# SP stores and loads k, then q, then the shift rows; a pair holds neighbouring heads; half of the output is normalised by one instruction

## The chip, the core and the metric

The kernel runs on one core of one Trainium2 chip. The metric is the device time of one execution in microseconds. The kernel before takes 1407.23 us, the median of 3 runs (1406.34 to 1412.29).

The engines have instruction queues of their own, which run in order and meet only at semaphores: PE (TensorE, matmuls, with its weight loads as PEld), DVE (VectorE), ACT (ScalarE), POOL (GpSimd) and SP (SyncE), which here issues every transfer. A queue whose next instruction waits holds up all that stands behind it.

## The reference

The input x is 32 batches of 256 rows and 256 columns, with a context of the same shape. The reference computes

```
x = x + tanh(g_xattn) * attention(layernorm(x), ctx)     # 16 heads of 16 columns, rope,
                                                          # |query - key| <= 50, softmax, Wo
x = x + tanh(g_ffn) * ffn(layernorm(x))                   # weights quantised in blocks of 32,
                                                          # activations rounded to 16 bits, I = 768
```

In the attention, q, k and v are projections with biases, q and k are rotated (rope), scores are divided by 4, and softmax runs over the 256 keys with all outside the band of 50 cut away. The result of each head stands at columns 16h to 16h+15 of the attention output before it is multiplied with Wo. The activation rounding of the feed-forward uses maxima over the whole tensor.

## The kernel before, in words

The program has three stages: `prepare` (weights quantised and transposed, some 60 us), `attention` (from there to about 830 us) and `feed_forward` (the rest). The change is in the first two.

**The attention is a pipeline over batches.** `run(steps)` writes out one unit after the other. In a unit, batch b0 is projected and rotated, b1 (the batch before) begins its scores, b2 does its weighting, b3 its output and b4 its second layer norm. A unit has 8 slots, and every engine has its own list of what it does in a slot, so the order on each engine is fixed by hand. Slot 3 of a unit begins the scores of b1 (`S_FIRST = 11`), slot 2 begins the transposed scores of b2 (`ST_FIRST = 18`), and the weighting of b2 starts in slot 5 (`PV_FIRST = 20`, done in twos).

**Heads go in pairs.** A pair is two heads of the stack, 2p and 2p+1. PE computes scores (`scores`, L835: q rows times k columns of a 96-row stack), DVE takes the row maxima (`maxima`, L707), then the maxima become *shift rows*, two more rows below q's stack (rows 96 and 97), and `scoresT` (L852) computes the scores again, transposed and with the maximum already taken away, by 98 rows. ACT takes the exponentials (L596), POOL cuts the band (L527, L536), and `weigh` (L878) multiplies with V.

**Where the stacks come from.** The rotated k and q are split into three bf16 parts each: ACT writes the high part (`high`, L581), DVE the remainder (L695), ACT the middle part (L587), and the low part is written by DVE for k and by POOL for q (both L415). SP then stores the 384 KB of parts to DRAM (`store_parts`, L451) and reads them back in another shape, 48 + 32 + 16 rows of 8 KB (`load_stacks`, L463, three transfers, 768 KB together). The load must wait for the landing of its store (`parts_stored`). The maxima of a half, 8 heads, go over PE and ACT (`shift_copy`, L608) to `shiftT`, and SP writes them below q's stack (`load_shift`, L471, two transfers of 4 KB). `scores` of pair 0 waits for both stacks (L828, L829), `scoresT` of pair 0 for shift half 0 and of pair 4 for shift half 1 (L847).

**What SP does in a unit**, in order: shift half 0 of b2, q's stack of b1, x and context of the next batch, the store of x2 (b4), x for the residual (b3), shift half 1 of b2, the stores of k and of q of b0, k's stack of b0. So q's parts are stored at the end of one unit and loaded at the start of the next, behind shift half 0.

**Which heads make a pair.** The columns of Wq, Wk and their biases are copied in `prepare` (L279, L289) so that stack head 2p is head p of the model and stack head 2p+1 is head p+8. `divide` then has the heads of both 128-column halves of the output in each half of its work: it takes a reciprocal (L732) and two multiplications (L739), one for each half of the columns, every second head of the bank each.

Of the kernel before, what the change touches and what calls it, by code (L numbers as in the profile page):

```python
# [12 lines left out]
ALU = mybir.AluOpType  # L13
# [5 lines left out]
P = 128  # L19
B, S, D = 32, 256, 256  # L20
H, DK = 16, 16
HALF = DK // 2
# [10 lines left out]
T = S // P  # L33
C = D // P
SPAN = P + WINDOW
FAR = S - SPAN
PAIRS = H // 2
SLOTS = PAIRS
NBUF = 3
HALVES = 2  # L40
# [8 lines left out]
VCOL = DK + 1  # L49
# [37 lines left out]
def prepare(nc, dram, w, banks, keep):  # L87

    with ExitStack() as ctx:
# [11 lines left out]
        qk_row, qk_row_dims = sb("qk_row", [1, 2, D]), sb("qk_row_dims", [1, 2, D])  # L101
# [169 lines left out]
        @block.scalar  # L271
        def _(act):

            act.wait_ge(bias_in, 112)
            for k in range(2):
                for o in range(T):

                    nc.scalar.activation(
                        qk_row_dims[:, k, :].rearrange("p (a d h o) -> p a d h o", a=2, d=HALF, h=PAIRS)[:, :, :, :, o],  # L279
                        qk_row[:, k, o * P:(o + 1) * P].rearrange("p (h a d) -> p a d h", h=PAIRS, a=2), ACT.Copy)\  # L280
                        .then_inc(qk_rows_made, 1)
            for k, blks in enumerate(plan):
                act.wait_ge(blocks_transposed, k + 1)
                at = place(blks)
                if blks[0][0] in ("Wq", "Wk"):

                    for q, (_, o, c, dst, _) in enumerate(blks):
                        last = nc.scalar.activation(
                            dst[0][:, c * D:(c + 1) * D].rearrange("p (a d h o) -> p a d h o", a=2, d=HALF, h=PAIRS)[:, :, :, :, o],  # L289
                            banks[k % 4][:, q * P:(q + 1) * P].rearrange("p (h a d) -> p a d h", h=PAIRS, a=2), ACT.Copy)  # L290
                    last.then_inc(bank_copied, 1)
                else:
                    nc.scalar.activation(blks[0][3][0][:, at:at + 4 * P], banks[k % 4][:], ACT.Copy).then_inc(bank_copied, 1)
                if k == len(attn) + 2:

                    act.wait_ge(out_bias_made, 1)
                    nc.scalar.activation(bpart[:, 0, :], banks[5][0:1, 0:D], ACT.Copy)
                    nc.scalar.activation(brow[:], banks[5][0:1, 0:D], ACT.Copy).then_inc(part_step, 1)
                if k > len(attn) + 2 and k <= len(attn) + 4:
                    m = k - len(attn) - 2  # L300
                    act.wait_ge(part_step, 2 * m)
                    nc.scalar.activation(bpart[:, m, :], (brest, brest2)[m - 1][:], ACT.Copy).then_inc(part_step, 1)
            act.wait_ge(blocks_transposed, len(plan) + 1)
            nc.scalar.activation(keep["qk_bias"][:], banks[6][:, 0:4], ACT.Copy).then_inc(bank_copied, 1)
            nc.scalar.activation(keep["tanh"][:], banks[4][:, 0:2], ACT.Tanh).then_inc(bank_copied, 1)
            act.wait_ge(bank_copied, len(plan) + 2)


def attention(nc, dram, x, ctx_in, scratch, banks, keep):

    with ExitStack() as ctx:
# [29 lines left out]
        att = sb("att", [P, T, D])  # L341
# [79 lines left out]
        @block.sync  # L421
        def _(sp):
            def load_x(b):
                if not b.real:
                    return

                reached(sp, x_transposed, b.before(1), 1, 1)
                sp.dma_start(x_in[:], rows_x[b.n]).then_inc(x_loaded, 16)
                reached(sp, c_transposed, b.before(1), 1, 1)
                sp.dma_start(c_in[:], rows_c[b.n]).then_inc(c_loaded, 16)  # L430

            def load_residual(b):
                if not b.real:
                    return

                bb = b.before(NBUF)
                if bb.n >= 0:
                    sp.wait_ge(x2_stored[b.buf], bb.rnd * 16 + 16)
                reached(sp, x2_normed, bb, T, T)
                sp.dma_start(x2[b.buf][:], rows_x[b.n]).then_inc(xres_loaded[b.buf], 16)  # L440

            def store_parts(b, n):
                if not b.real:
                    return

                reached(sp, mid_ready[n], b, 1, 1)
                reached(sp, low_ready[n], b, 1, 1)

                if b.n >= NBUF:
                    sp.wait_ge(stack_loaded[n][b.buf], b.rnd * 48)  # L450
                sp.dma_start(scratch[n][b.buf].rearrange("k (a d) (h t) -> (d h) (k a) t", a=2, h=H),  # L451
                             parts[n][:].rearrange("p k (a t) -> p (k a) t", a=2)).then_inc(parts_stored[n], 16)

            def load_stacks(b, n):
                if not b.real:
                    return
                stack = (q_stack if n == "q" else k_stack)[b.buf]
                reached(sp, parts_stored[n], b, 16, 16)
                reached(sp, scoredT, b.before(NBUF), 2 * PAIRS, 2 * PAIRS)
                row = 0  # L460
                for g in range(3):
                    rows = (3 - g) * DK
                    sp.dma_start(stack[row:row + rows, :, :].rearrange("r s t -> r (s t)"), scratch[n + "_rows"](b.buf, g)).then_inc(stack_loaded[n][b.buf], 16)  # L463
                    row += rows

            def load_shift(b, half):
                if not b.real:
                    return
                reached(sp, shiftT_copied, b, HALVES, half + 1)
                for k in range(SHIFT):  # L470
                    sp.dma_start(q_stack[b.buf][STACK + k:STACK + k + 1, half * 8:half * 8 + 8, :],  # L471
                                 shiftT[half][k * 8:(k + 1) * 8, :]).then_inc(shift_loaded[half][b.buf], 16)

            def store_x2(b):
                if not b.real:
                    return
                reached(sp, x2_ready, b, 1, 1)
                sp.dma_start(scratch["x2"][b.n], x2[b.buf][:]).then_inc(x2_stored[b.buf], 16)

            def steps(rnd, unit):  # L480
                load_shift(Batch(rnd, unit, 2), 0)
                load_stacks(Batch(rnd, unit, 1), "q")
                load_x(Batch(rnd, unit, -1))
                store_x2(Batch(rnd, unit, 4))
                load_residual(Batch(rnd, unit, 3))
                load_shift(Batch(rnd, unit, 2), 1)
                store_parts(Batch(rnd, unit, 0), "k")
                store_parts(Batch(rnd, unit, 0), "q")
                load_stacks(Batch(rnd, unit, 0), "k")

            run(steps)
            for k in range(NBUF):
                sp.wait_ge(x2_stored[k], 16 * len(range(k, B, NBUF)))
# [168 lines left out]
        def _(dve):  # L662
# [62 lines left out]
            def divide(b, half):  # L725

                if not b.real:
                    return
                reached(dve, out_transposed, b, HALVES, half + 1)
                src = out_bank[half][:].rearrange("p (t s d) -> p t s d", t=T, d=OUT)  # L730
                mine = rden[:, :, half * PAIRS:(half + 1) * PAIRS]
                nc.vector.reciprocal(mine, src[:, :, :, DK]).then_inc(rden_ready, 1)  # L732
                reached(dve, rden_ready, b, HALVES, half + 1)
                reached(dve, att_transposed, b.before(1), 1, 1)
                heads = PAIRS // HALVES
                for c in range(C):

                    at = c * P + half * heads * DK
                    ins = nc.vector.tensor_tensor(  # L739
                        att[:, :, at:at + heads * DK].rearrange("p t (h d) -> p t h d", d=DK), src[:, :, c::2, 0:DK],  # L740
                        mine[:, :, c::2].unsqueeze(3).to_broadcast([P, T, heads, DK]), ALU.mult)
                ins.then_inc(out_normed, 1)

            def residual(b):
                if not b.real:
# [46 lines left out]
        def _(pe):  # L792
# [65 lines left out]
            def weigh(b, pair, later):  # L858
# [14 lines left out]
                for e in range(2):  # L873
                    h = 2 * pair + e
                    row = (h % 4) * OUT
                    for c in range(T):
                        v_at = (c * H + h // 2 + PAIRS * (h % 2)) * VCOL
                        last = nc.tensor.matmul(out_bank[half][row:row + OUT, col + c * FAR:col + c * FAR + SPAN],  # L878
                                                V[b.buf][:, v_at:v_at + OUT], ring_tile(probs, b, pair, c)[:, e, :],
                                                start=(c == 0), stop=(c == T - 1), skip_group_check=True)  # L880
# [840 lines left out]
```

## Time and profile before

| | us |
|---|---|
| median of 3 runs | 1407.23 |
| the profiled execution | 1405.53 |
| its span | 1403.8 |
| PE busy | 1195.9 (85%) |
| DVE busy | 1202.3 (86%) |
| ACT busy | 837.5 (60%) |
| POOL busy | 587.1 (42%) |

The span is from the first to the last instruction; 1.7 us lie around it. Busy is the time in which an engine had an instruction under way, matmuls with their modelled ends. DVE and PE are both busy for most of the span, so the attention is read from what either waits for in one unit. The granted clock of PE is 0.94 over the span: in some stretches PE runs at half speed. SP's instructions count as busy on no engine, its waits are read from the timeline of its queue.

### The profile page before, as it was taken

How to read it: one execution, taken by the hardware profiler on the slowest of the kernel's cores; microseconds unless marked ns; L12 is line 12 of the kernel's file. 1: busy time of each engine (PE TensorE's matmuls, PEld its weight loads, DVE VectorE, ACT ScalarE, POOL GpSimd, SP SyncE). 2: the span in 40 equal slices, each digit the busy share in tenths (PEclk: the TensorE clock that was granted, in tenths of full speed). 3: DMA queues.
4: the chain of work that ended last, by engine and by line, in shares of the span. 5: the costliest groups of instructions: out<-in, count | busy, mean ns of one | idle time of the engine just before them, and what ended most of it. 6: DMA issues, size and time to landing. Idle time of an engine off the chain costs nothing. (4 is left out here: it accounts for less than half of the span.)

```text
span 1403.8 us, 27833 instructions
## 1 busy us (share of the span) xinstructions
PE 1195.9 (85%) x8960; PEld 807.6 (58%) x8992; DVE 1202.3 (86%) x3570; ACT 837.5 (60%) x1336; POOL 587.1 (42%) x1392
## 2 busy tenths in 40 slices
PE   3367898988888888888888767999899979977998
PEld 2245676776766766666676543444333334436887
DVE  5678998999999899899989736998899989997886
ACT  2225665656666565657565545664676779993332
POOL 1127787778778787778777640000000000000000
PEclk7679999999999999999999988999999999998999
DMA  3174856566666667575757311222455455556774
GB/s 113 34 161 108 180 137 159 137 159 148 149 157 149 153 144 158 138 158 139 169 127 170 85 38 45 112 91 111 151 188 187 170 179 193 188 179 203 234 237 164
DMA packets 132369, 207.27 MB, mean 148 GB/s; under 512 B 11159, under 2 KB 97050, under 8 KB 126106
## 3 DMA queue, kind: packets, MB, share of 16 engines
q1 hardware_dynamic: 132250, 205.86, 53.6%
q8 instruction: 53, 0.87, 0.3%
q14 instruction: 66, 0.54, 0.1%
HBM read 125.60 MB, written 79.69 MB: 146 GB/s over the span
## 5 line engine op out<-in xcount | busy, mean ns | idle before, releaser
L596 ACT ACTIVATE probs<-psum 128x356 f32<-128x356 f32 x512 | 210.2, 464 | 246.4 <-PE psum L852 246.4
L707 DVE CUSTOM_DVE_ANT_0 psum<-psum,band 128x178 f32<-128x178 f32 x1024 | 317.2, 372 | 40.1 <-PE psum L835 38.5
L1014 PE MATMUL psum<-xnT,w_upT 128*128 (+1 forms) x1152 | 260.8, 384 | 19.1 <-DVE maxima L1238 8.8
L527 POOL TENSOR_SCALAR_AFFINE_SELECT probs<-probs 128x154 f32<-128x154 f32 (+1 forms) x512 | 214.3, 426 | 146.9 <-ACT probs L596 141.0
L835 PE MATMUL psum<-k_stack,q_stack 96*128 96x178 bf16 x1024 | 143.2, 251 | 88.0 <-issue 57.2
L1014 PEld LDWEIGHTS psum<-xnT,w_upT 128*128 128x128 f16 x1152 | 109.7, 99 | 170.0 <-issue 32.2
L536 POOL TENSOR_SCALAR_AFFINE_SELECT probs<-probs 128x254 f32<-128x254 f32 (+1 forms) x512 | 189.1, 393 | 0.0
L835 PEld LDWEIGHTS psum<-k_stack,q_stack 96*128 96x128 bf16 x1024 | 76.5, 100 | 145.4 <-issue 86.6
L707 DVE DVE_READ_ACCUMULATOR2_ANT smax<- 128x1 f32 x1024 | 142.7, 139 | 0.0
L1614 PE MATMUL psum<-w_downT,xnT 128*128 128x256 f16 x1152 | 128.1, 275 | 16.0 <-DVE xnT L1564 16.0
L1014 PE MATMUL psum<-xnT,w_gateT 128*128 (+1 forms) x576 | 125.9, 382 | 8.7 <-DVE xnT L1087 8.7
L1614 PEld LDWEIGHTS psum<-w_downT,xnT 128*128 128x128 f16 x1152 | 113.8, 99 | 30.6 <-DVE xnT L1564 16.5
L852 PE MATMUL psum<-q_stack,k_stack 98*128 98x178 bf16 x1024 | 126.7, 247 | 2.5 <-DMA q_stack<-shiftT 1.2
L878 PE MATMUL psum<-probs,V 128*32 128x178 f32 x2048 | 113.0, 334 | 1.9 <-POOL probs L536 1.7
L1014 PEld LDWEIGHTS psum<-xnT,w_gateT 128*128 128x128 f16 x576 | 56.6, 98 | 77.9 <-DVE xnT L1087 9.1
L852 PEld LDWEIGHTS psum<-q_stack,k_stack 98*128 98x128 bf16 x1024 | 90.1, 100 | 13.5 <-issue 1.5
L1589 ACT ACTIVATE xnT<-xnT 128x1536 f16<-128x1536 int16 x32 | 47.5, 1484 | 80.7 <-DVE xnT L1545 80.7
L878 PEld LDWEIGHTS psum<-probs,V 128*32 128x32 f32 x2048 | 66.7, 113 | 13.6 <-POOL probs L536 2.1
L1275 ACT ACTIVATE sig<-inner_int,scales 128x1536 f32<-128x1536 int16 x32 | 50.5, 1577 | 40.3 <-DVE maxima L1244 40.2
L810 PE MATMUL psum<-WoT,attT 128*128 128x256 f32 x256 | 62.1, 387 | 7.9 <-ACT attT L567 5.5
L810 PE MATMUL psum<-WvT,cT 128*128 128x256 f32 x256 | 68.1, 413 | 0.0
L819 PE MATMUL psum<-cT,WkT 128*128 128x256 f32 x256 | 65.6, 402 | 0.0
(189 smaller groups left out, 2283.7 us busy)
## 6 DMA issues: line engine op xcount, KB each, us to landing
k_parts_scratch<-k_parts SPq DMA_DIRECT2D x32, 384.0 KB, 2.6
q_parts_scratch<-q_parts SPq DMA_DIRECT2D x32, 384.0 KB, 2.6
k_stack<-k_parts_scratch SPq DMA_DIRECT2D x32, 384.0 KB, 5.1
q_stack<-q_parts_scratch SPq DMA_DIRECT2D x32, 384.0 KB, 6.0
gate_scratch<-g_stage SPq DMA_DIRECT2D x16, 768.0 KB, 3.3
g_in<-gate_scratch SPq DMA_DIRECT2D x16, 768.0 KB, 4.6
sig_scratch<-w_gateT SPq DMA_DIRECT2D x32, 384.0 KB, 2.3
sig_again<-sig_scratch SPq DMA_DIRECT2D x32, 384.0 KB, 3.4
```

The lines of the kernel that those rows point to most:

```text
L527: nc.gpsimd.affine_select(out=t[:, :, 0:n], in_=t[:, :, 0:n], pattern=[[0, 2], [1, n]], compare_op=ALU.is_ge, fill=0.0, base=WINDOW - off, ...
L536: nc.gpsimd.affine_select(out=t[:, :, n:SPAN], in_=t[:, :, n:SPAN], pattern=[[0, 2], [-1, SPAN - n]], compare_op=ALU.is_ge, fill=0.0, base ...
L596: nc.scalar.activation(ring_tile(probs, b, pair, c)[:].rearrange("p e j -> p (e j)"), scoreT_bank[c][:, 0:2 * SPAN], ACT.Exp, scale=DK ** ...
L707: ins = nc.vector.tensor_tensor_reduce(out=mine, in0=mine, in1=keep["band"][:, t, :], scale=1.0, scalar=-3e38, op0=ALU.add, op1=ALU.max, a ...
L810: last = nc.tensor.matmul(out, srcT[:, c, t * P:(t + 1) * P], weight[:, c * D:(c + 1) * D], start=(c == 0 and not biased), stop=(c == C - ...
L819: last = nc.tensor.matmul(bank[:, half * S:(half + 1) * S], weight[:, c * D + half * P:c * D + (half + 1) * P], srcT[:, c, :], start=(c == ...
L835: last = nc.tensor.matmul(bank[:, e * SPAN:(e + 1) * SPAN], q_stack[b.buf][0:STACK, h, t * P:(t + 1) * P], k_stack[b.buf][0:STACK, h, t * ...
L852: last = nc.tensor.matmul(scoreT_bank[c][:, e * SPAN:(e + 1) * SPAN], k_stack[b.buf][0:STACK + SHIFT, h, c * P:(c + 1) * P], q_stack[b.buf ...
L878: last = nc.tensor.matmul(out_bank[half][row:row + OUT, col + c * FAR:col + c * FAR + SPAN], V[b.buf][:, v_at:v_at + OUT], ring_tile(probs ...
L1014: last = nc.tensor.matmul(bank[:], weights[wp][:, c * I + f * P:c * I + (f + 1) * P], x_parts[:, c, bass.ds(j * (2 * TILE) + xp * TILE, TI ...
L1275: nc.scalar.activation(sig[h][:], kept(j, h), ACT.Sigmoid, scale=col(G_S)).then_inc(sig_done, 1)
L1614: last = nc.tensor.matmul(bank[:, 0:D], o[odd][f // HF][op][:, at:at + P], keep["w_downT"][wp][:, f * D:(f + 1) * D], start=(f == 0 and k ...
```

## The change

Four places change.

- In `prepare`, the columns of Wq, Wk and their biases keep the order of the model: stack heads 2p and 2p+1 are heads 2p and 2p+1 of the model. The same number of ACT copies, with another stride on the destination.
- In `weigh`, V is read at the head's own place.
- In `divide`, the 8 heads of a half are now 128 neighbouring columns, and one multiplication over 128x256 elements takes the place of two over 128x128.
- In SP's `steps`, each stack is loaded directly behind its own store, k before q, and shift half 0 comes behind q's load, still in the same unit.

```diff
@@ prepare, biases and weights of q and k
-  qk_row_dims[:, k, :].rearrange("p (a d h o) -> p a d h o", ...)[:, :, :, :, o],
+  qk_row_dims[:, k, :].rearrange("p (a d o h) -> p a d h o", ...)[:, :, :, :, o],
...
@@ SP
             def steps(rnd, unit):
-                load_shift(Batch(rnd, unit, 2), 0)
-                load_stacks(Batch(rnd, unit, 1), "q")
                 load_x(Batch(rnd, unit, -1))
                 store_x2(Batch(rnd, unit, 4))
                 load_residual(Batch(rnd, unit, 3))
                 load_shift(Batch(rnd, unit, 2), 1)
-                store_parts(Batch(rnd, unit, 0), "k")
-                store_parts(Batch(rnd, unit, 0), "q")
-                load_stacks(Batch(rnd, unit, 0), "k")
+                for n in "kq":
+                    store_parts(Batch(rnd, unit, 0), n)
+                    load_stacks(Batch(rnd, unit, 0), n)
+                load_shift(Batch(rnd, unit, 1), 0)
@@ DVE, divide
-                heads = PAIRS // HALVES
-                for c in range(C):
-                    at = c * P + half * heads * DK
-                    ins = nc.vector.tensor_tensor(
-                        att[:, :, at:at + heads * DK].rearrange("p t (h d) -> p t h d", d=DK), src[:, :, c::2, 0:DK],
-                        mine[:, :, c::2].unsqueeze(3).to_broadcast([P, T, heads, DK]), ALU.mult)
-                ins.then_inc(out_normed, 1)
+                nc.vector.tensor_tensor(
+                    att[:, :, half * P:(half + 1) * P].rearrange("p t (s d) -> p t s d", d=DK), src[:, :, :, 0:DK],
+                    mine.unsqueeze(3).to_broadcast([P, T, PAIRS, DK]), ALU.mult).then_inc(out_normed, 1)
@@ PE, weigh
-                        v_at = (c * H + h // 2 + PAIRS * (h % 2)) * VCOL
+                        v_at = (c * H + h) * VCOL
```

On SP, one unit of the steady part of the attention, before, from the store of k's parts to the next one. `k_parts_scratch` is k's parts in DRAM, `q_stack<-shiftT` the two transfers of a half of the shift rows; the first such row here is half 0, the second half 1.

```order
L451 DMA k_parts_scratch<-k_parts 128x6x256
L451 DMA q_parts_scratch<-q_parts 128x6x256
L463 DMA k_stack<-k_parts_scratch 48x1x4096
L463 DMA k_stack<-k_parts_scratch 32x1x4096
L463 DMA k_stack<-k_parts_scratch 16x4096
L471 DMA q_stack<-shiftT 1x8x256 x2
L463 DMA q_stack<-q_parts_scratch 48x1x4096
L463 DMA q_stack<-q_parts_scratch 32x1x4096
L463 DMA q_stack<-q_parts_scratch 16x4096
L428 DMA x_in<-in_x 128x2x256
```

The same stretch on SP in the changed kernel, beginning with the same store.

```order
L451 DMA k_parts_scratch<-k_parts 128x6x256
L463 DMA k_stack<-k_parts_scratch 48x1x4096
L463 DMA k_stack<-k_parts_scratch 32x1x4096
L463 DMA k_stack<-k_parts_scratch 16x4096
L451 DMA q_parts_scratch<-q_parts 128x6x256
L463 DMA q_stack<-q_parts_scratch 48x1x4096
L463 DMA q_stack<-q_parts_scratch 32x1x4096
L463 DMA q_stack<-q_parts_scratch 16x4096
L471 DMA q_stack<-shiftT 1x8x256 x2
L428 DMA x_in<-in_x 128x2x256
```

k's load has moved in front of q's store, and the shift rows have moved from in front of q's load to behind it. The rest of the unit stands in the same order in both.

On DVE, the normalisation of one half in slot 2, before: between the last product of k's rope and the first maxima.

```order
L684 SCALAR_TENSOR_TENSOR k_cos<-psum,qk_bias,cos 128x256
L686 SCALAR_TENSOR_TENSOR k_sin<-psum,qk_bias,sin 128x256
L732 RECIPROCAL rden<-psum 128x2x8
L739 TENSOR_TENSOR att<-psum,rden 128x2x64 x2
L707 ISA psum,smax<-psum,band 128x178
```

The same place on DVE in the changed kernel, where the lines are one and five lower.

```order
L683 SCALAR_TENSOR_TENSOR k_cos<-psum,qk_bias,cos 128x256
L685 SCALAR_TENSOR_TENSOR k_sin<-psum,qk_bias,sin 128x256
L731 RECIPROCAL rden<-psum 128x2x8
L734 TENSOR_TENSOR att<-psum,rden 128x2x128
L706 ISA psum,smax<-psum,band 128x178
```

Two instructions have become one of twice the size; nothing else on DVE has moved.

## Rows read from the trace of the kernel before

**Rows 1.** Windows: attention from batch 0's first scores to batch 31's; engines, PEclk, DMA share, GB/s.
```profile
83.88:793.40 709.52, 615.28 (x5646) 478.22 (x5676) 639.60 (x2912) 440.27 (x989) 547.23 (x1291) 0.96 0.65 149
```

**Rows 2.** Waits of PE, 120 to 760 us: total us, times, longest.
```profile
PE psum L835 <- issue: 51.2, 28, 3.1
```

**Rows 3.** Timeline of PE: start, us, instruction, [idle before it <- what ended it].
```profile
83.88 0.75 PE L835 MATMUL psum<-k_stack,q_stack 96*128 96x178 bf16 x4 [4.66 <-DMA q_stack<-q_parts_scratch]
...
334.23 0.47 PE L835 MATMUL psum<-k_stack,q_stack 96*128 96x178 bf16 x4 [1.97 <-issue]
...
335.81 0.48 PE L835 MATMUL psum<-k_stack,q_stack 96*128 96x178 bf16 x4
...
354.49 0.47 PE L852 MATMUL psum<-q_stack,k_stack 98*128 98x178 bf16 x4
357.01 0.47 PE L835 MATMUL psum<-k_stack,q_stack 96*128 96x178 bf16 x4 [2.04 <-issue]
```

**Rows 4.** Timeline of SP: k's load of one unit, then the whole of the next.
```profile
321.99 2.47 SPq L463 DMA_DIRECT2D k_stack<-k_parts_scratch  x3
...
339.12 0.37 SPq L451 DMA_DIRECT2D k_parts_scratch<-k_parts  x1
344.24 0.37 SPq L451 DMA_DIRECT2D q_parts_scratch<-q_parts  x1
344.70 1.87 SPq L463 DMA_DIRECT2D k_stack<-k_parts_scratch  x3
346.61 1.39 SPq L471 DMA_DIRECT2D q_stack<-shiftT  x2
348.10 1.84 SPq L463 DMA_DIRECT2D q_stack<-q_parts_scratch  x3
349.99 0.42 SPq L428 DMA_DIRECT2D x_in<-in_x  x1
...
362.31 0.37 SPq L451 DMA_DIRECT2D k_parts_scratch<-k_parts  x1
```

**Rows 5.** L463, three transfers issued from 348.1: last start, then time to landing.
```profile
L463 SPq DMA_DIRECT2D q_stack<-q_parts_scratch x3: 575/592/592, 348.1 to 349.4; - x3
DMA to landing us min/median/max: 6.1/6.8/7.6
```

**Rows 6.** Median time to landing, whole span: transfer, count, KB, us.
```profile
k_parts_scratch<-k_parts SPq DMA_DIRECT2D x32, 384.0 KB, 2.6
k_stack<-k_parts_scratch SPq DMA_DIRECT2D x32, 128.0 KB, 6.0
q_stack<-q_parts_scratch SPq DMA_DIRECT2D x32, 128.0 KB, 6.9
x_in<-in_x SPq DMA_DIRECT2D x32, 256.0 KB, 6.9
```

**Rows 7.** Windows around a store of parts, columns as in rows 1.
```profile
344.00:345.00 1.00, 1.00 (x7) 0.87 (x6) 1.00 (x8) 0.04 (x1) 1.00 (x4) 1.00 0.00 0
345.00:346.00 1.00, 1.00 (x17) 0.74 (x19) 1.00 (x6) 0.49 (x2) 0.46 (x2) 1.00 0.92 281
```

**Rows 8.** L463, k's stack of the last batch, and PE's timeline behind it.
```profile
L463 SPq DMA_DIRECT2D k_stack<-k_parts_scratch x3: 567/591/607, 781.2 to 782.5; - x3
DMA to landing us min/median/max: 5.1/5.9/6.1
789.07 0.48 PE L852 MATMUL psum<-q_stack,k_stack 98*128 98x178 bf16 x4 [1.19 <-DMA q_stack<-shiftT]
```

**Rows 9.** Timeline of DVE: first maxima of pair 1, slot 4.
```profile
336.35 0.34 DVE L707 CUSTOM_DVE_ANT_0 psum<-psum,band 128x178 f32<-128x178 f32 x1
```

**Rows 10.** Timeline of ACT: exponentials of pair 0.
```profile
354.85 0.82 ACT L596 ACTIVATE probs<-psum 128x356 f32<-128x356 f32 x2 [2.42 <-PE psum L852]
```

**Rows 11.** L739, all of it: ns min/median/max; and the nearest PSUM form of 256 elements.
```profile
L739 DVE TENSOR_TENSOR att<-psum,rden x128: 280/286/292, 121.4 to 829.2; 128x128 f32<-128x128 f32 x128
L684 DVE SCALAR_TENSOR_TENSOR k_cos<-psum,qk_bias,cos 128x256 f32<-128x256 f32 x2 | 1.0, 481 | 1.0 <-PE psum L819 1.0
```

More of the change, by code:

```diff
@@ L278, in _ @@
                     nc.scalar.activation(
-                        qk_row_dims[:, k, :].rearrange("p (a d h o) -> p a d h o", a=2, d=HALF, h=PAIRS)[:, :, :, :, o],
+                        qk_row_dims[:, k, :].rearrange("p (a d o h) -> p a d h o", a=2, d=HALF, h=PAIRS)[:, :, :, :, o],
                         qk_row[:, k, o * P:(o + 1) * P].rearrange("p (h a d) -> p a d h", h=PAIRS, a=2), ACT.Copy)\
@@ L288, in _ @@
                         last = nc.scalar.activation(
-                            dst[0][:, c * D:(c + 1) * D].rearrange("p (a d h o) -> p a d h o", a=2, d=HALF, h=PAIRS)[:, :, :, :, o],
+                            dst[0][:, c * D:(c + 1) * D].rearrange("p (a d o h) -> p a d h o", a=2, d=HALF, h=PAIRS)[:, :, :, :, o],
                             banks[k % 4][:, q * P:(q + 1) * P].rearrange("p (h a d) -> p a d h", h=PAIRS, a=2), ACT.Copy)
```

## The prediction

> **What bounds the kernel now.** I first read the busy time over the part of the attention in which the pipeline is full, from the first scores of batch 0 to those of batch 31 [rows 1]: 709.5 us for 31 batches, so one batch every 22.9 us. PE is busy for 615 of it and DVE for 640, that is 19.8 and 20.6 us a batch. Both are nearly full and neither is full: about 2 us a batch go elsewhere. Second, PE's own waits [rows 2]: 51.2 us in 28 pieces, one for each of 28 batches, 1.8 us each, all ahead of L835. The profile calls their cause "issue", so I looked for it in the timeline. There the wait stands ahead of `scores` of pair 0 [rows 3], which needs both stacks. The last transfer of q's stack is issued at 349.4 and lands 7.6 us later, at 357.0 [rows 5], and PE begins at 357.01. Batch 0 has the same wait with its cause named, DMA q_stack. So the "issue" is the landing of q's stack.
>
> This closes a loop. From PE's start on a batch's scores, DVE, ACT and POOL need a fixed time until the parts of the next batch are ready (q's are stored at 344.24, 10.0 us after 334.23); from q's store to the landed stack it is 12.7 us [rows 3, 4]. The sum is 22.7 and the next scores begin at 357.01, 22.8 after the last. What counts for the change is therefore how long SP's chain is, not what any engine saves.
>
> **The half instruction on DVE.** 64 reciprocals stay; 128 multiplications of 286 ns become 64 of twice the elements. Two take 572 ns now. One of 256 elements costs between 286 (as if size were free) and 481 ns, the nearest form that reads PSUM with as many elements [rows 11]. I take 420, nearer to the upper row, so DVE gains 0.15 us each half, 0.3 a batch, at most 18 us over all (bounds 6 and 18). None of it is on the chain: the first half is normalised ahead of the point at which PE waits, the second behind k's low part. I count 0; what hides it is PE's wait for the stack. If that wait were gone, it would be worth some 5 to 10 us.
>
> **The neighbouring heads.** The same copies in `prepare` with another stride, the same matmuls with V read elsewhere. At most 16 small ACT copies could change by a fraction of their time; 0.
>
> **SP's order: what it removes.** q's load is no longer issued behind k's load and the shift rows. In the unit shown it is issued 3.4 us after k's and 3.9 us after its own store [rows 4], though the store lands after 2.6 [rows 6]. About 1.3 us could be saved if nothing else changed.
>
> **SP's order: what it adds.** Two things. k's load now stands ahead of q's store on SP and in the transfer queue, and the queue runs dry between the two loads. And shift half 0 stands behind q's load, while `scoresT` of pair 0 (L852), which needs it, comes ahead of `scores` of pair 0 in PE's order (354.49 and 357.01 [rows 3]). Behind the waiting L852 stand L835 and all of slot 3, and for them wait DVE and ACT. So the chain now ends at L852. I add it up from the issue of k's store.
>
> - k's store lands: 2.6 [rows 6]. Only then is k's load issued. SP is free well before q's parts are ready (5.1 us behind k's [rows 4]), so SP itself isn't the trouble.
> - k's load into an empty queue. Before, its last transfer starts 1.3 us after its first and lands 6.0 later, 7.3 in all [rows 4, 6], with q's store ahead of it. That store is issued at 344.24, nothing moves until 345 and then 0.92 of the queue is busy at 281 GB/s [rows 7]: it starts some 0.9 after its issue, and 384 KB take about 1.3. k's load, issued 0.46 later, thus waited about 0.8; alone it would need 6.5. Some groups of three take 2.5 instead of 1.9 us to issue [rows 4], which adds to the end, so I take 6.7. Bounds: not under 0.9 plus 4.3, the distance of the landings of the two loads when they follow one another (3.4 + 1.3 + 6.9 - 7.3 [rows 4, 6]), so 5.2; not over 7.9, as with a store ahead and the slow issue.
> - q's store goes through the queue behind k's load. x_in, issued 1.9 after q's load began, lands 6.9 later, q's last transfer 1.3 + 6.9: x_in lands 0.6 behind it [rows 4, 6]. x_in is 256 KB, the store 384 KB: 1.1, with bounds of 0.5 and 2.6 (as from an empty queue).
> - q's load again into an empty queue: 6.7.
> - the shift rows behind it, until L852 runs: 0.5. In the last batch k's stack lands at 782.5 + 6.1 = 788.6 and L852, which waits for the shift rows behind it, starts at 789.07 [rows 8].
> - L852 to L835 of pair 0: 0.4 (four matmuls of one group, 0.47 [rows 3]).
> - L835 to the next store of k: 4.9 and 5.3 in the two units shown (334.23 to 339.12, 357.01 to 362.31 [rows 3, 4]), so 5.1.
> - what the later L852 adds to this: ACT starts the exponentials 0.36 after it and needs 0.82 for two [rows 10]; pair 1's second half waits for them, 0.5 later than L852 now comes. PE reaches pair 1's scores 1.58 after pair 0's now, DVE takes their maxima at 336.35, 0.54 behind PE's start [rows 3, 9], of which 0.35 is what DVE always needs. 0.3 is left over (bounds 0 and 0.6).
>
> Sum: 2.6 + 6.7 + 1.1 + 6.7 + 0.5 + 0.4 + 5.1 + 0.3 = 23.4 us a batch, against 22.9. PE's idle time per batch grows and moves from L835 to L852. Times 31 batches it is +16 us; the profiled execution took 1405.5, so 1421.5, and the median lies 1.7 above that execution: 1423. The feed-forward isn't touched.
>
> **A rule weighed.** The landing of k's store after 2.6 us for 1.3 us of moving shows that much of a small transfer is neither moving nor waiting for others. The Trainium skill (DMA: Bandwidth & Descriptors, "Anatomy of one DMA — SWDGE (gpsimd) path") gives a transfer a fixed 2.0 us, most of it the receipt of the last byte, and 436 GB/s beyond, and by it serial hand-offs, of which this change makes one more, each pay the 2 us. By the same rule a stack of 768 KB alone would land 3.8 us after its issue, the chain would be 17.6 us, and the kernel would be bound by its engines, as in the rival below. The rows don't bear that out: two loads back to back land 4.3 us apart [rows 4, 6], more than the rule's whole price for one.
>
> **The rivals.**
>
> *Faster, by a short chain.* With q's store not held behind k's load (landing 2.6 after its issue, since its packets might slip between the 8 KB rows), or with loads of 5.5 us in the emptier queue, the chain is 23.4 less 2.4: 21.0. Then the engines bind: 22.9 less PE's 1.8 is 21.1. That gives -1.8 x 31 = -56 us, 1351. Halfway, with loads of 6.1 us each, it is 22.2 a batch, -22, 1385. For it: before, the queue is idle at times (share 0.00 at 344 [rows 7], 0.65 on average [rows 1]) and now has less in it. Against it: x_in lands behind the stack it was issued behind, in order. It decides at a load of 6.4 us. Chance 0.22 with the halfway case, of it 0.02 for loads of 3.8.
>
> *No change.* The two effects cancel: loads of 6.4 to 6.6 us, or the shift rows landing earlier. Chance 0.18, 1407. It also takes in that SP's new order never reaches the critical chain.
>
> *Much slower.* The exponentials of pair 0 come late, POOL's cut of it comes ahead of q's rotation on its queue, and PE, idle longer in one piece, gets the lower of its clock's two levels (1.2 GHz of 2.4) more often; the granted clock is already 0.96 on average [rows 1]. With 0.6 for the one and 0.5 for the other the batch takes 24.5: +50, 1457. It begins to decide where q's low part isn't ready before k's stack has landed, and that has 3 us of room (10.6 + 1.2 against 5.8 + 2.6 + 6.7 from L852). Chance 0.12.
>
> **How the numbers follow.** The forecast has 0.48, with a range of its own of 1413 to 1440 (loads of 6.5 to 7.0). A measurement of this kernel tells 0.5%, 7 us, from no change. Slower: 0.48 and 0.12, 0.60. Same 0.18, faster 0.22. The range leaves out the full engine-bound case and the far end of the much slower one: 1385 to 1450.
>
> **What would show it.** Right: SP's timeline has k's load 2.6 us behind k's store and q's load some 8 us behind that; q's store lands 4 to 5 us after its issue instead of 2.6; PE's idle time of 2 to 3 us stands ahead of L852, released by the shift rows, and none to speak of ahead of L835; one batch takes 23 to 24 us; L734 takes some 420 ns and DVE's sum is 5 to 10 us lower with no effect. Wrong: q's store still lands after 2.6 us; or k's load after under 6.4 us; or L835 still waits, with the shift rows there before L852 is due.

## The result and the profile after

The changed kernel takes 1449.22 us (median of 4 runs, 1448.37 to 1453.28) against 1408.14 for the kernel before on the same chips. The ratio is 1.0293, with a 95% interval of 1.0263 to 1.0324: 2.9% slower, 41 us. The forecast was 1423 (+16 us), with a range of 1385 to 1450. So the time lies just inside the far end of the range, and the loss is 2.6 times the one forecast.

Over the same part of the attention as in [rows 1], batch 0's first scores to batch 31's, the window has the start and end, its length, the busy time of PE, PEld, DVE, ACT and POOL, the granted clock, the transfer share and GB/s:

```profile
87.36:837.92 750.56, 636.51 (x5646) 486.29 (x5676) 637.12 (x2853) 432.38 (x988) 541.23 (x1287) 0.93 0.60 141
```

750.6 us for 31 batches where [rows 1] has 709.5: 24.2 us a batch instead of 22.9, and these 41.0 us are all but the whole of the loss (the span grew by 42.9). DVE's busy time is 2.5 us less than before. The granted clock is 0.93 instead of 0.96. The queue of transfers is less busy, 0.60 instead of 0.65.

PE's waits, as in [rows 2] (total us, times, longest), from 120 to 800 us:

```profile
PE psum L846 <- DMA q_stack<-shiftT: 64.7, 26, 4.1
PE psum L829 <- DVE smax L706: 11.3, 42, 0.3
...
PE psum L846 <- issue: 4.3, 2, 2.3
```

The wait has moved from `scores` of pair 0 (L835, now L829) to `scoresT` of pair 0 (L852, now L846), which waits for the shift rows, and has grown from 1.8 to 2.5 us (64.7/26). Ahead of L829 little is left but DVE's maxima. SP's timeline of one unit, against [rows 4]:

```profile
360.07 0.37 SPq L451 DMA_DIRECT2D k_parts_scratch<-k_parts  x1
362.64 1.86 SPq L463 DMA_DIRECT2D k_stack<-k_parts_scratch  x3
365.19 0.37 SPq L451 DMA_DIRECT2D q_parts_scratch<-q_parts  x1
370.15 2.37 SPq L463 DMA_DIRECT2D q_stack<-q_parts_scratch  x3
372.57 1.39 SPq L471 DMA_DIRECT2D q_stack<-shiftT  x2
...
383.26 0.37 SPq L451 DMA_DIRECT2D k_parts_scratch<-k_parts  x1
```

k's load goes out 2.6 us behind k's store, as forecast. q's store goes out when POOL is ready, 5.1 behind k's store, and SP then waits 5.0 us for it, until 370.15. The time to landing of the two loads in this unit (the last of three starts at 363.9 and 371.4), and the end of the chain in PE's timeline:

```profile
L463 SPq DMA_DIRECT2D k_stack<-k_parts_scratch x3: 566/587/607, 362.6 to 363.9; - x3
DMA to landing us min/median/max: 4.9/5.4/5.5
```

```profile
L463 SPq DMA_DIRECT2D q_stack<-q_parts_scratch x3: 548/587/1139, 370.2 to 371.4; - x3
DMA to landing us min/median/max: 5.5/6.0/6.2
```

```profile
377.66 0.48 PE L846 MATMUL psum<-q_stack,k_stack 98*128 98x178 bf16 x4 [2.05 <-DMA q_stack<-shiftT]
377.98 0.47 PE L829 MATMUL psum<-k_stack,q_stack 96*128 96x178 bf16 x4
378.55 0.69 PE L846 MATMUL psum<-q_stack,k_stack 98*128 98x178 bf16 x4
```

k's stack lands at 363.9 + 5.5 = 369.4, q's store 0.7 behind it, q's stack at 371.4 + 6.2 = 377.6, and L846 starts at 377.66. The last row is the late exponentials: pair 1's transposed scores need 0.69 us for four matmuls instead of 0.47, since the second half waits for ACT. PE's weight loads show that wait (120 to 800 us); the kernel before has none there:

```profile
PEld psum L846 <- ACT probs L595: 10.4, 42, 0.3
```

Medians of the whole span, against [rows 6]; the 128.0 KB are the third transfer of a stack, the 16 rows:

```profile
k_parts_scratch<-k_parts SPq DMA_DIRECT2D x32, 384.0 KB, 2.6
...
q_parts_scratch<-q_parts SPq DMA_DIRECT2D x32, 384.0 KB, 5.5
...
k_stack<-k_parts_scratch SPq DMA_DIRECT2D x32, 128.0 KB, 5.5
q_stack<-q_parts_scratch SPq DMA_DIRECT2D x32, 128.0 KB, 5.7
```

The multiplication of 256 elements took what was chosen from [rows 11]:

```profile
L734 DVE TENSOR_TENSOR att<-psum,rden x64: 423/424/425, 128.8 to 873.7; 128x256 f32<-128x256 f32 x64
```

It saves less than was forecast all the same. The two multiplications before overlap. The second starts 208 ns after the first, and from the start of the first to the end of the second it is 488 ns, not 572. The groups of the whole span show it, before and after (busy us, then mean ns of one):

```profile
L739 DVE TENSOR_TENSOR att<-psum,rden 128x128 f32<-128x128 f32 x128 | 31.3, 286 | 2.2
L734 DVE TENSOR_TENSOR att<-psum,rden 128x256 f32<-128x256 f32 x64 | 27.1, 424 | 2.2
```

That is 0.06 us a half and 4.2 us in all, where the forecast had 0.15 a half.

### The profile page after: what moved, and what is told of

It is laid out like the page before. It is cut to its first block and busy times, and to the rows that moved or that the text cites. A ratio compares the mean times of both kernels' runs of the same rounds, so it can differ in the third digit from the quotient of the medians.

```text
span 1446.7 us, 27769 instructions
## 1 busy us (share of the span) xinstructions
PE 1212.9 (84%) x8960; PEld 812.2 (56%) x8992; DVE 1199.3 (83%) x3506; ACT 830.2 (57%) x1336; POOL 583.7 (40%) x1392
## 5 line engine op out<-in xcount | busy, mean ns | idle before, releaser
L526 POOL TENSOR_SCALAR_AFFINE_SELECT probs<-probs 128x154 f32<-128x154 f32 (+1 forms) x512 | 197.6, 396 | 193.1 <-ACT probs L595 188.5
L846 PE MATMUL psum<-q_stack,k_stack 98*128 98x178 bf16 x1024 | 138.3, 258 | 81.1 <-DMA q_stack<-shiftT 74.6
L535 POOL TENSOR_SCALAR_AFFINE_SELECT probs<-probs 128x254 f32<-128x254 f32 (+1 forms) x512 | 197.3, 409 | 0.0
L829 PE MATMUL psum<-k_stack,q_stack 96*128 96x178 bf16 x1024 | 145.8, 256 | 27.5 <-DVE smax L706 18.2
L846 PEld LDWEIGHTS psum<-q_stack,k_stack 98*128 98x128 bf16 x1024 | 88.0, 103 | 111.4 <-DMA q_stack<-shiftT 83.5
L829 PEld LDWEIGHTS psum<-k_stack,q_stack 96*128 96x128 bf16 x1024 | 82.9, 103 | 77.7 <-DVE smax L706 40.9
L872 PE MATMUL psum<-probs,V 128*32 128x178 f32 x2048 | 118.0, 347 | 1.9 <-POOL probs L535 1.7
```

The lines of the kernel that those rows point to most:

```text
L526: nc.gpsimd.affine_select(out=t[:, :, 0:n], in_=t[:, :, 0:n], pattern=[[0, 2], [1, n]], compare_op=ALU.is_ge, fill=0.0, base=WINDOW - off, ...
L535: nc.gpsimd.affine_select(out=t[:, :, n:SPAN], in_=t[:, :, n:SPAN], pattern=[[0, 2], [-1, SPAN - n]], compare_op=ALU.is_ge, fill=0.0, base ...
L829: last = nc.tensor.matmul(bank[:, e * SPAN:(e + 1) * SPAN], q_stack[b.buf][0:STACK, h, t * P:(t + 1) * P], k_stack[b.buf][0:STACK, h, t * ...
L846: last = nc.tensor.matmul(scoreT_bank[c][:, e * SPAN:(e + 1) * SPAN], k_stack[b.buf][0:STACK + SHIFT, h, c * P:(c + 1) * P], q_stack[b.buf ...
```

## The experiments

All have the new heads unless it is said. The ratios are to the kernel before, from runs on the same chip; experiments 1 to 4 share one chip, 5 and 6 another, 7 and 8 a third. "Stores first" is the old order k, q, then the loads. The diffs are shortened, and `b0` in them stands for `Batch(rnd, unit, 0)`. PE's waits are from 120 to 760 us unless it is said.

**1. The heads and the single multiplication alone** (SP's order of the kernel before).

```diff
-                for n in "kq":
-                    store_parts(Batch(rnd, unit, 0), n)
-                    load_stacks(Batch(rnd, unit, 0), n)
-                load_shift(Batch(rnd, unit, 1), 0)
+                store_parts(b0, "k"); store_parts(b0, "q"); load_stacks(b0, "k")
+                load_shift(Batch(rnd, unit, 1), 0); load_stacks(b0, "q")
```

> SP's old order with the new head pairs, V places and the single multiplication. Theory (all of the loss is SP's chain, the wait for the stacks hides DVE's gain): 1407 us, at most 4 off, the loop still 22.9 to 23.0 us a batch, L835 of pair 0 still waits 1.8 us for q's stack. Rival (the neighbouring heads cost something, in V's reads or in the strided work): most of the 41 us, so 1430 or more. Second rival (DVE bounds it after all): 10 us of DVE gained show, 1397.

Measured: 1408.79 us, ratio 1.0005 (0.9983 to 1.0026). PE's waits:

```profile
PE psum L830 <- issue: 50.9, 28, 3.3
```

That is the old row, 51.2 us in 28 pieces. The heads and the single multiplication together are worth nothing that these runs can tell (the interval goes from 2 us faster to 4 slower), and the loss is SP's order.

**2. Stores first, shift half 0 behind q's load.**

```diff
+                store_parts(b0, "k"); store_parts(b0, "q"); load_stacks(b0, "k")
+                load_stacks(b0, "q"); load_shift(Batch(rnd, unit, 1), 0)
```

> New heads; both stores first as in the kernel before (k, q), then k's load, q's load, and shift half 0 behind q's load as in the changed kernel. It takes away the hand-offs in series and keeps the place of the shift rows. Theory (both parts cost): L852 waits for the shift rows behind q's load, L835 comes 0.56 later than with a wait of its own and the late exponentials and the clock cost 0.6 more: 24.0 us a batch, 1440 us. Rival (only the series of hand-offs costs): 1407. Rival (only the place of the shift rows costs): 1449.

Measured: 1443.13 us, ratio 1.0227 (1.0178 to 1.0275).

```profile
PE psum L847 <- DMA q_stack<-shiftT: 55.3, 24, 3.4
PE psum L830 <- DVE smax L707: 9.3, 35, 0.3
```

Against experiment 1 nothing but this one step has moved, and 34 of the 41 us are lost already (the interval of the ratio leaves some 7 us either way). q's load is issued earlier here than in either kernel, 3.0 us behind q's store (4.3 before, 5.4 in the changed kernel), and it doesn't help: it follows k's in the queue, and the stack lands 12.5 to 12.6 us behind q's store in all three.

**3. Series of hand-offs, shift half 0 ahead of q's load.**

```diff
+                store_parts(b0, "k"); load_stacks(b0, "k"); store_parts(b0, "q")
+                load_shift(Batch(rnd, unit, 1), 0); load_stacks(b0, "q")
```

> New heads; SP as in the changed kernel (store k, load k, store q, load q) but shift half 0 between q's store and q's load, where SP only waits for the landing of the store. It keeps the hand-offs in series and gives L852 its rows early. Theory: PE waits ahead of L835 again, the chain loses 0.56 + 0.6 of its 24.4: 23.2 us a batch, 1414 us. Rival (only the series costs): 1449. Rival (only the place of the shift rows costs): 1407.

Measured: 1417.26 us, ratio 1.0049 (1.0025 to 1.0072).

```profile
PE psum L830 <- issue: 52.7, 27, 3.7
86.62:807.23 720.61, 630.46 (x5675) 488.22 (x5676) 640.58 (x2853) 439.57 (x989) 547.71 (x1291) 0.94 0.63 147
```

The second row is the window from batch 0's first scores to batch 31's. PE waits for q's stack again (1.95 us each), a batch takes 23.2, as expected. The series by itself costs 8 us (experiment 3 less 1), the place of the shift rows 34 (experiment 2 less 1), and together with the 1408.8 of experiment 1 they would give 1452: the changed kernel has 1449.2. The two add up, as far as these runs can tell.

**4. q's store on a queue of ACT's.** SP as in 3 without the store; in ACT's slot 7:

```diff
+                        if b0.real:
+                            reached(act, low_ready["q"], b0, 1, 1)
...
+                            nc.scalar.dma_start(scratch["q"][b0.buf]..., parts["q"][:]...).then_inc(parts_stored["q"], 16)
```

> As the kernel with shift half 0 ahead of q's load, but q's store is issued by ACT (slot 7, ahead of the exponentials, where ACT idles) on a queue of its own. Theory (q's store lands 5.4 us after its issue instead of 2.6 because it lies behind k's load in one queue; k's load can go early for nothing if the store needn't follow it): q's store lands after 3 to 3.5, q's load goes into a queue with little of k's load left, chain 10.3 + 3.3 + 7.0 = 20.6, the engines bind at 21.1 to 21.8 a batch, 1355 to 1375 us, faster than both. Rival (the transfer engines, not the queue, hold the store up): it lands after 5 as before, 1410.

Measured: 1413.58 us, ratio 1.0025 (1.0004 to 1.0046). The theory fell. The queues and the landing of the store:

```profile
q1 hardware_dynamic: 107162, 193.27, 48.8%
q10 hardware_dynamic: 25088, 12.58, 3.7%
...
q_parts_scratch<-q_parts ACTq DMA_DIRECT2D x32, 384.0 KB, 5.5
```

The store went through a queue of its own (q10, 12.58 MB) and still took 5.5 us to land, as in the changed kernel. So it isn't the order within one queue that holds it behind k's load. The Trainium skill (DMA: Bandwidth & Descriptors, "Queues, rings and completion order") has all queues on the same 16 engines, each taking turns between them, and a completion that lands only after that engine's earlier writes; the 5.5 us agree with shared engines. The packets in the traces say what holds the store: on the queue of its own its first packet starts 2.46 us after its issue (mean of the fourth to the twenty-ninth batch), in experiment 3, on the load's queue, 2.43, and in the kernel before, with no load ahead, 0.91. So the data itself moves late, whichever queue it is on, and for these 2.4 to 2.5 us it is packets of the load that go on starting. A turn for the store's packets from its issue on is not to be seen.

**5. q's parts in two steps.**

```diff
+                store_parts(b0, "k")
+                store_q(b0, 0, 2)            # high and middle part, waits for mid_ready
+                load_stacks(b0, "k")
+                store_q(b0, 2, 3)            # low part, waits for low_ready
+                load_q(b0, (0, 1))           # 48 and 32 rows
+                load_shift(Batch(rnd, unit, 1), 0)
+                load_q(b0, (2,))             # 16 rows
```

> New heads. q's high and middle parts (256 KB) are stored as soon as ACT has the middle one, some 4 us before POOL has the low one, and the low part (128 KB) by itself; of q's stack the 48 and 32 rows of the first two parts are loaded behind k's load without waiting for the low part, then shift half 0, then the last 16 rows (128 KB). Theory (the loop is q's low part, its store, the wait behind k's load, q's load into an empty queue, L835): q's last rows land some 3.5 us earlier than in the kernel before, 9 us behind the low part's store, the chain is 10.3 + 9.1 = 19.4 and the engines bind at 21.1 to 21.8 us a batch, 1350 to 1375 us; PE's idle time ahead of L835 all but goes. Rival (the bytes and the engines' sharing set it, since the batch moves as much as before): 1400 or more.

Measured: 1376.31 us, ratio 0.9748 (0.9710 to 0.9785); in a second session (below) 1377.91. It is 2.4 to 2.5% faster than the kernel before and 5% faster than the changed one.

```profile
PE psum L856 <- DVE smax L733: 40.4, 140, 0.6
PE psum L819 <- ACT cT L591: 4.5, 28, 0.2
PE psum L856 <- issue: 2.6, 3, 1.4
PE psum L873 <- DMA q_stack<-shiftT: 2.1, 3, 1.3
PE psum L873 <- issue: 2.0, 1, 2.0
```

These are from 120 to 800 us. The window from batch 0's first scores to batch 31's:

```profile
83.31:766.09 682.78, 619.42 (x5676) 460.84 (x5676) 640.65 (x2853) 435.04 (x989) 545.24 (x1290) 0.99 0.66 155
```

PE's waits for the stacks and the shift rows (the last three rows) have shrunk from 51 to under 7 us with the same bytes moved (384 + 768 KB for q), so bytes aren't the limit but the order in which they become ready. PE now begins the scores of pair 0 1.1 us behind q's landing on average, 0.09 before. The batch takes 22.0 us, at a granted clock of 0.99. The median lies 1 us beyond the slower end of what I had written, since a batch takes 22.0 us and not at most 21.8.

**6. The changed kernel with its wait filled.** In `scoresT`, ahead of the wait of pair 0:

```diff
+                if pair == 0:
+                    reached(pe, exp_done, b, 2 * PAIRS, -1)
+                    for _ in range(12):
+                        nc.tensor.matmul(scoreT_bank[0][:, 384:512], ident[:], ident[:], start=True, stop=True)
```

> The changed kernel, with 12 more matmuls of 128x128 f32 on PE ahead of the wait of L852 of pair 0 for the shift rows; they write columns of a bank that nobody reads and take some 1.8 us of the 2.5 that PE idles there. Theory (of the 0.8 us by which a batch got slower than forecast, 0.4 to 0.5 is PE at the lower clock after the longer idle time: 18 falls of the clock in 26 batches after, 11 before, and 0.77 us from L835 to k's store in such a batch): falls of the clock under 5 in 26 batches, L835 to k's store 5.3 instead of 5.8 us, 1433 us. Rival (the low clock only goes with late batches and isn't their cause): falls go and the time stays at 1449.

Measured: 1440.57 us, ratio 1.0197 (1.0156 to 1.0238), 8.7 us less than the changed kernel with more work on PE. The two medians are from different chips; by the ratios to the kernel before (1.0293 for the changed one) it is 13 us less, and the two intervals don't meet. One window of this kernel and of the changed one, 130 to 780 us (the columns as above; the clock is the third number from the end):

```profile
130.00:780.00 650.00, 615.48 (x5757) 489.45 (x5757) 553.35 (x2513) 385.82 (x888) 485.10 (x1161) 1.00 0.61 144
```

```profile
130.00:780.00 650.00, 556.48 (x4999) 426.58 (x5028) 554.31 (x2480) 384.72 (x879) 480.67 (x1145) 0.94 0.60 141
```

The clock stays at its upper level (one fall in 26 batches in its record, 18 in the changed kernel). From L829 of pair 0 to k's next store it takes 5.32 us on average instead of 5.83, as much as in those batches of the changed kernel in which the clock stays up (5.29). So the low clock is a cause of lost time. Of the 16 us expected between half and four fifths came back. The 12 matmuls, 24 instructions in the trace, are drawn out over 2.8 us, more than the 1.8 I had reckoned, and where the shift rows came earlier PE was late itself (0.46 us from q's landing to L850 on average, 0.21 in the changed kernel); q's low part came 0.3 us later against k's.

**7. and 8. Is the single multiplication worth something once the stacks no longer bind?** Experiment 5 with the old heads and two multiplications, and experiment 5 once more beside it.

> SP as in the kernel that stores q in two steps, but with the old pairs of heads and two multiplications of 286 ns for each half. In the kernel with the new ones DVE is no longer held by the stacks' landing. Theory (the single multiplication saves 0.15 us twice a batch, and counts as soon as DVE sets the pace): 5 to 10 us slower than that kernel, 1381 to 1386. Rival (DVE's saving is covered by PE or ACT here too): the same time, within 2 us.

> The kernel that stores q in two steps, with the new pairs and the single multiplication, once more on the same chip as the one with the old pairs: 1376 us, within 3.

Measured: 1377.27 with the old heads, ratio 0.9757 (0.9733 to 0.9781); 1377.91 with the new, ratio 0.9761 (0.9736 to 0.9786). The same time; the theory fell. DVE's waits from 130 to 760 us, old heads first, then new:

```profile
DVE k_cos L710 <- PE psum L845: 27.3, 28, 1.0
DVE psum L733 <- PE psum L861: 1.1, 1, 1.1
```

```profile
DVE k_cos L710 <- PE psum L840: 27.3, 28, 1.0
DVE psum L733 <- PE psum L856: 1.2, 2, 0.9
```

In both, DVE waits 0.97 us a batch for k's projection on PE, and nearly every batch takes 22.14 us. So DVE doesn't set the pace there by itself. There was also less to save than I had taken: 0.06 us a half is 4 us over all, and DVE's busy time from 130 to 760 us is 594.2 us with the old heads and 595.2 with the new. I have not settled which steps of PE and DVE make up these 22.14.

## Why the prediction was right in its way and wrong in its size

The direction and the mechanism hold, and experiments 1 to 3 show them one at a time: the DVE part is worth nothing, the wait moves to L852, and SP's order costs. The size was 41 us where I had 16. The sum of the prediction had eight terms; the table takes the last two together. The means over 26 batches, the fourth to the twenty-ninth, from the start or landing of each instruction in the trace:

| term | forecast | measured |
|---|---|---|
| k's store lands | 2.6 | 2.75 |
| k's load, issue to landing | 6.7 | 6.98 |
| q's store behind it | 1.1 | 1.05 |
| q's load, issue to landing | 6.7 | 7.14 |
| shift rows, to the start of L852 | 0.5 | 0.21 |
| L852 to L835 | 0.4 | 0.44 |
| L835 to k's next store, late exponentials with it | 5.4 | 5.83 |
| sum | 23.4 | 24.4 |

Over all 31 batches it is 24.2, and 22.9 before.

**The step that failed** is the size of two kinds of term in this sum. The two loads into an empty queue went in at 6.7 each and took 6.98 and 7.14: 0.7 of the 1.0 us by which the sum was short. The stretch "L835 to the next store of k: ... so 5.1", with 0.3 for the later L852, took 5.83: 0.4 of it.

**The stretch.** In the batches in which the clock stayed up, the stretch took 4.99 before and 5.29 after: the 0.3 for the exponentials was right. In the batches in which it fell, 5.54 before and 6.06 after, and these were 11 of 26 before and 18 of 26 after. I had seen the fall, PEclk 0.96 [rows 1], and put it into the "much slower" rival alone, with its chance of 0.12. But that PE would idle longer at one point followed from the forecast itself. So the clock belonged in the sum. It is 0.23 us a batch before and 0.53 after, each from one execution. The number of falls differs between executions too: experiment 1, with SP's old order and the same wait of 1.8 us, has 6 in 26. The rest of the 0.4 is the 5.1 itself, read from two units, where the mean before was 5.22. Experiment 6 shows that the clock is a cause: without the falls the stretch takes 5.32 and the kernel is some 9 us faster.

**The loads** were each taken 0.3 to 0.4 too short. The 7.3 for k's load before was a sum of two medians, 1.3 and 6.0. From the start of its first transfer to the landing of its last the mean over the 26 batches is 7.67, and a chain pays the mean; with that and the 0.8 of waiting taken off, the load alone would have come to 6.9. Late issues, for which the forecast had added 0.2, are not what remains: in the changed kernel they are 1 of 26 groups of k's and 3 of 26 of q's. Why q's load takes 7.14 there is open. Together, 0.7 of loads, 0.4 of the stretch and 0.15 of the store, less 0.3 of the shift rows, make the 1.0 us a batch by which the sum was short. That is 31 us on the sum, and the loss was only 25 us over the forecast because the batches at either end are quicker than the 26.

**Point by point.** That k's load goes out 2.6 us behind k's store, q's load some 8 (7.5 in the unit shown) behind that: right. That q's store lands 4 to 5 us after its issue: later, 5.5 at the median (4.9 in the unit shown). That one batch takes 23 to 24 us: a little more, 24.2. That DVE's work falls by 5 to 10 us with no effect: its busy time over the whole span falls by 1.8 us in experiment 1 and 3.0 in the changed kernel, no effect. The step behind it, "Two take 572 ns now", was wrong: they take 488. That the single multiplication "would be worth some 5 to 10 us" once the wait is gone: wrong, experiments 7 and 8. That the engines bind at 21.1 us (22.9 less the wait): wrong, in experiment 5 the wait is all but gone and it is 22.0. PE then waits more for DVE's maxima (120 to 760 us, before and in experiment 5):

```profile
PE psum L835 <- DVE smax L707: 16.1, 62, 0.3
PE psum L856 <- DVE smax L733: 38.4, 135, 0.3
```

That is 0.8 us a batch more, about the 0.9 that is missing; that it is the cause is not shown. The rival with 3.8 us for a load, by the price of the Trainium skill (DMA: Bandwidth & Descriptors, "Anatomy of one DMA — SWDGE (gpsimd) path") for one transfer, is refuted by 7.0.

**The rival "much slower"** came nearest in time, 1457 with 24.5 us a batch, but not by its own steps. Its clock came true in part (0.3 us more a batch, where it had 0.5), the exponentials cost the 0.3 of the forecast and not another 0.6, and q's low part was ready in time: q's store went out 5.4 us behind k's store on average, while k's stack lands 9.7 behind it.

**The rival of a short chain** rested on q's store slipping between the rows of k's load. It lands behind them, 1.05 after, and does so on a queue of its own too (experiment 4, 25 of 26 batches).

**What I hadn't seen at all** is that the two halves of SP's change have such different weights. I added both into one chain. The series of hand-offs costs 8 us: q's load goes out 5.4 us behind q's store instead of 4.1 (experiments 3 and 1), but into an empty queue, and lands 7.3 after its issue instead of 8.4, so most of the delay is won back. The place of the shift rows costs 34: by the rows of experiment 2 it makes PE start L835 0.57 us later behind q's landing (0.66 instead of 0.09), and the stretch from L835 to k's next store takes 5.91 instead of the 5.12 of experiment 1. Of these 0.8 some 0.35 stand in batches with the clock up as well (5.37 against 5.02), the late exponentials; the rest goes with 22 falls of the clock in 26 batches instead of 6.

## What to carry to other kernels

Where two transfers gate two instructions of one in-order queue, the small one that gates the earlier instruction goes first; behind a long load it delays everything that stands in between, at a price many times its bytes. When a forecast says that TensorE idles longer, its clock is a term of the sum and not a rival: count the falls and what a fall costs in the trace of before. And what stands last in a chain should be little: here the part that is ready last is a third of the store and a sixth of the load, and giving it a hand-off of its own brought 2.4%.

## What the runs showed of the hardware that I had not expected

A store of 384 KB issued while a load of 768 KB is under way lands after 5.5 us instead of 2.6, on the load's own queue as well as on another engine's (5.5 both times), and its first packet starts 2.4 to 2.5 us after its issue instead of 0.9. Two multiplications on DVE of 286 ns each take 488 ns together, and one of twice the elements 424. A piece of PE work of 12 matmuls, 2.8 us long, keeps the granted clock at 1.00 where an idle time of 2.5 us on average brings it to 0.94 over the stretch, and a kernel with this useless work is some 9 us faster than the same one without (13 by the ratios).
